# One more, smaller group in a grouped pipeline: images in groups of 2, 2, 6 x 4, 2, 2 instead of 2, 7 x 4, 2

## The chip, the cores and the metric

The kernel runs on one core of a Trainium2 chip, as one launch. The metric is the device time of that launch in microseconds (us), as the median over several runs. An engine is called here by the profile's name: PE (TensorE), DVE (VectorE), ACT (ScalarE), POOL (GpSimd), SP (SyncE). An image has 68 positions (36 patches and 32 text tokens) of 256 features; 32 images make 2176 rows, which are 17 tiles of 128 rows.

## The reference, cut to what matters

Four layers with residual sums: windowed attention, a mixture of 64 experts with 8 chosen per row, a layer that mixes the positions of an image by a learned causal roll, and a mixture of 8 experts with one chosen per row. The change lies in the third layer, which is this:

```python
z = softmax(einsum('bse,he->bsh', x, W_A) * SCALING, axis=1)     # per image and head, over positions
roll = transpose(z)[:, :, (i - j) % S] * (j <= i)                # causal roll
v = einsum('bse,fe->bsf', x, W_V).reshape(B, S, H, D)
out = einsum('bhij,bjhd->bihd', roll, v).reshape(B, S, E)
h = h + einsum('bse,fe->bsf', out, W_O) + b_O                    # x is layernorm(h)
```

The kernel computes the roll as a convolution: a discrete Fourier transform over the 68 positions of an image (two real matrices, `fwd`), products with the transform of z, and the inverse (`inv`). Ahead of it stands the end of the second layer: each row of h gets the weighted sum of the 8 rows that its experts left in memory. Behind it stand the layernorm and the 8 router logits of the fourth layer.

## The kernel before, in words

The third layer is one function, `roll_layer` (from line 1503), with an instruction list of its own for each engine, and every wait is written out by hand. The 32 images are cut into groups (`SIZES`, line 1510: 2, then seven times 4, then 2). All five engines go through the same rounds i = 0, 1, ..., `STEPS` - 1, where `STEPS` is the number of groups and three more (12 before). In round i

- group i is collected: DVE adds the 8 expert rows to each tile (`combine`, line 1948) and measures it for the layernorm (`measure`);
- group i-1 is normalised by ACT, transposed by PE (`turn("in")`, line 1635), and gets its logits z (`mix_logits`, 1643), its values v (`values`, 1654, one pair of images at a time), the softmax over z (`mix_shift` and `mix_norm` on DVE) and the transform of z (`turn_mix`, `forward_mix`);
- group i-2 gets the transform of v (`forward`, line 1663, two matmuls per pair), the products (`multiply`, line 2008, on DVE), the inverse (`invert`, line 1690) and the projection (`project`, line 1701);
- group i-3 gets the residual sum, the second layernorm, a transpose (`turn("out")`, also line 1635) and the router logits (`choose`, line 1736), and SP stores its tiles (lines 1599 and 1600).

Images don't end where tiles do. A group collects the tiles that its last image reaches (`tiles_in`), and hands out the tiles that are then complete (`tiles_out`). Before, `tiles_in` is 0 1 | 2 3 | 4 5 | 6 7 | 8 9 | 10 11 | 12 13 | 14 15 | 16, and `tiles_out` is 0 | 1 2 | 3 4 | 5 6 | 7 8 | 9 10 | 11 12 | 13 14 | 15 16.

POOL issues the 136 gathers of the expert rows (line 1623), 8 per tile in order of tiles, whatever the groups are. The buffer holds four tiles, so the gathers of tile t wait for the sums of tile t-4. In its first gathers POOL also waits for the end of the second layer's shared expert, whose last 9 tiles PE, ACT and DVE work off before round 0.

DVE, in a round (lines 2031 to 2077): the scale of the "in" norm, the residual sum, the "out" measures, the products of the first pair, the scale of the "out" norm, the bias, the sums of all collected tiles but the last, the softmax's shift, the products of the second pair, the softmax's norm, and at the end the sums of the last collected tile. PE, in a round (lines 1766 to 1825): the forward transforms, matmuls on idle data that only keep it running (`fill`, line 1712: 6 in a steady round of 4 images, 20 in rounds 1 and 2), the "in" transposes, logits, values, the "out" transposes, values of the second pair, router logits, the two inverses, `turn_mix`, `project`, `forward_mix`. Outside the steady rounds (`steady(g)`: 1 < g < NG - 1) there are more such idle matmuls (`fill_mid`, `fill_values`).

SP issues four loads of 1 MiB of the fourth layer's weights ahead of the stores of group 4 (`if g == 4`, line 1593), that is once the tiles of group 3 are out. The fourth layer begins when all engines have left the block.

Of the kernel before, what the change touches and what calls it, by code (L numbers as in the profile page):

```python
# [851 lines left out]
def attention_and_mixture_0(nc, a, k):  # L852

    with ExitStack() as st:
        sb = lambda n, s, d=fp32: k["sb"](f"m0_{n}", s, d, st)
        x_rows = nc.dram_tensor("m0_x_rows", (T, D), fp32).ap()
        y_rows = nc.dram_tensor("m0_y_rows", (SLOTS0 * P, D), fp32).ap()
        coef = sb("coef", [P, NT, E0])
        ids = sb("ids", [P, SLOTS0], u32)
        tile_expert_row = sb("tile_expert_row", [1, 2 * P], i32)  # L860
        r = places(k, st, "m0", E0, K0, SLOTS0)
        shared_up, shared_down = sb("shared_up", [P, DC, 2 * D]), sb("shared_down", [P, DC, D])
        with ExitStack() as js:
            jb = lambda n, s, d=fp32: k["sb"](f"m0_{n}", s, d, js)
            m = dict(coef=coef, ids=ids, tile_expert_row=tile_expert_row, x_rows=x_rows,
                     router=jb("router", [P, DC, E0]), e_bias=jb("e_bias", [P, E0]),
                     up=shared_up, down=shared_down)
            m["routing_in"], = sems(nc, k, "m0j", "routing_in")
            aT = jb("aT", [P, DC, T])
            wo = jb("wo", [P, DC, D])  # L870
            window_attention(nc, a, k, m, aT, wo)
            join_and_route(nc, k, m, r, aT, wo)
        wt = sb("wt", [P, NT, K0])
        expert_tiles_0(nc, a, k, ids, tile_expert_row, x_rows, y_rows, r, coef, wt)
        clear_sems(nc, k)
        roll_layer(nc, a, k, r, wt, y_rows, shared_up, shared_down)
# [626 lines left out]
def roll_layer(nc, a, k, r, wt, y_rows, shared_up, shared_down):  # L1503
# [3 lines left out]
    fwd = [k["const"]("fwd_re"), k["const"]("fwd_im")]  # L1507
    inv = [k["const"]("inv_re"), k["const"]("inv_neg"), k["const"]("inv_im"), k["const"]("inv_im")]
    GI, PAIR = 4, 2
    SIZES = [2] + [4] * 7 + [2]  # L1510
    assert sum(SIZES) == B
    NG = len(SIZES)
    FROM = [sum(SIZES[:g]) for g in range(NG + 1)]
    GC = GI * S
# [13 lines left out]
    def halves(g):  # L1528
        return range(SIZES[g] // PAIR)

# [6 lines left out]
    def cols_of(g):  # L1537
        return slice(FROM[g] * S, FROM[g + 1] * S)
# [13 lines left out]
    with ExitStack() as st:  # L1552
# [35 lines left out]
        with nc.Block() as block:  # L1588
# [39 lines left out]
            def _(pe):  # L1628
# [9 lines left out]
                def mix_logits(g):  # L1638
# [3 lines left out]
                    for c in range(DC):  # L1642
                        mm = nc.tensor.matmul(pz[0:H, 0:SIZES[g] * S], late["w_a"][:, c, :], xT[:, c, cols_of(g)],
                                              start=(c == 0), stop=(c == DC - 1))
# [21 lines left out]
                def turn_mix(g):  # L1666
                    pe.wait_ge(z_normed, g + 1)
                    for b in range(SIZES[g]):
                        mm = nc.tensor.transpose(pz[0:S, b * H:(b + 1) * H], z[:, b, :], ident[0:H, 0:H])
# [814 lines left out]
```

## Time and profile before

| | us |
|---|---|
| median of 3 runs | 1057.34 (1054.91 to 1061.70) |
| the profiled execution, its own time | 1059.86 |
| its span | 1058.10 |
| PE busy in the span | 947.0 (90%) |
| DVE busy | 589.4 (56%) |
| POOL busy | 520.6 (49%) |
| roll layer, first gather to the router logits on DVE | 626.1 to 860.1 |

Times in the rows below are counted from the start of the span. A row of a timeline reads: start, duration, engine, line, operation, output tile <- input tiles, shape, how many instructions are merged; in square brackets the engine's idle time just before it and what ended that. PEclk is the clock that PE was granted: 1.00 is 2.4 GHz, 0.50 is 1.2 GHz.

### The profile page before, as it was taken

Reading aid. Unit: us, or ns where it says so; the run is one execution under the profiler, and the core shown is the slowest. Engines: PE = TensorE matmul, PEld = TensorE weight load, DVE = VectorE, ACT = ScalarE, POOL = GpSimd, SP = SyncE. Lnnn points to the kernel's source line nnn. Section 1 sums busy time; section 2 is a strip of 40 time slices with the busy share of each in tenths; the row PEclk is TensorE's granted clock in tenths of the full one; section 3 lists DMA queues with packets and bytes.
Section 4 is the critical chain, followed back from the end, with each engine's and each line's share of the span. In section 5 each row is a group of like instructions: output and inputs, shape, how many; then the busy total and the mean of one; then the engine's idle time right before and its main releaser. Section 6 shows DMA issues by size and latency. Waiting matters only on the chain. (4 is left out here: it accounts for less than half of the span.)

```text
span 1058.1 us, 29663 instructions
## 1 busy us (share of the span) xinstructions
PE 947.0 (90%) x10380; PEld 745.1 (70%) x10398; DVE 589.4 (56%) x1463; ACT 413.5 (39%) x1102; POOL 520.6 (49%) x714
## 2 busy tenths in 40 slices
PE   8899999988747999999999998789888957999996
PEld 6667777777634888888888876355556635888895
DVE  1778888865994777433333325676887551111111
ACT  2267677734243344444443422222333222333431
POOL 0055665610604777777777627777772002433432
PEclk9999999999969999999999999887999987999998
DMA  7010000002004888877788723344483056476650
GB/s 256 1 46 2 0 0 0 1 12 75 1 1 161 292 283 261 272 247 224 242 265 253 230 89 100 100 113 122 122 289 80 21 191 218 143 262 222 266 155 25
DMA packets 79820, 149.28 MB, mean 141 GB/s; under 512 B 18892, under 2 KB 53327, under 8 KB 75760
## 3 DMA queue, kind: packets, MB, share of 16 engines
q1 hardware_dynamic: 34768, 77.15, 21.7%
q0 software_dynamic: 17712, 47.88, 16.0%
q10 hardware_dynamic: 27248, 23.09, 6.5%
q8 instruction: 50, 0.82, 0.3%
q14 instruction: 42, 0.34, 0.1%
HBM read 200.22 MB, written 31.73 MB: 219 GB/s over the span
## 5 line engine op out<-in xcount | busy, mean ns | idle before, releaser
L1332 POOL DMA_INDIRECT x_x<-m_x_rows,x_idx x170 | 165.7, 975 | 75.1 <-issue 35.6
L1358 PE MATMUL x_pup<-x_xt,x_w 128*128 128x128 f32 (+1 forms) x2176 | 182.9, 250 | 0.0
L1358 PEld LDWEIGHTS x_pup<-x_xt,x_w 128*128 128x128 f32 (+1 forms) x2176 | 166.9, 165 | 5.9 <-issue 5.7
L1623 POOL DMA_INDIRECT rl_y<-m_y_rows,rl_idx x136 | 134.2, 986 | 43.6 <-issue 36.3
L1439 DVE TENSOR_TENSOR x_hid<-x_gate,x_pup 128x128 f32<-128x128 f32 x170 | 48.9, 288 | 148.3 <-ACT x_gate L1411 140.9
L1372 PE MATMUL x_pdown<-x_w,x_hid 128*128 128x256 f32 (+1 forms) x408 | 104.2, 389 | 0.3 <-DVE x_y L1446 0.3
L1407 ACT ACTIVATE x_xt<-x_pturn 128x256 f32<-128x256 f32 x170 | 65.3, 384 | 89.3 <-PE x_pturn L1343 86.2
L442 POOL TENSOR_TENSOR wa_probs<-wa_probs,wa_peak 68x544 f32<-68x544 f32 x64 | 69.9, 1092 | 57.6 <-DVE wa_peak L593 54.9
L2420 DVE TENSOR_TENSOR x_y<-x_pdown,x_b 128x256 f32<-128x256 f32 x21 | 8.9, 425 | 151.7 <-PE x_pdown L2374 151.7
L2406 ACT ACTIVATE x_hid<-x_pup,x_b 128x128 f32<-128x128 f32 (+1 forms) x200 | 52.8, 357 | 95.9 <-PE x_pup L2357 95.8
L1411 ACT ACTIVATE x_gate<-x_pup 128x128 f32<-128x128 f32 x170 | 47.2, 278 | 92.4 <-PE x_pup L1358 91.7
L1953 DVE SCALAR_TENSOR_TENSOR h<-rl_y,m_wt,h 128x256 f32<-128x256 f32 x136 | 66.2, 487 | 18.1 <-DMA rl_y<-m_y_rows,rl_idx 13.8
L1446 DVE COPY x_y<-x_pdown 128x256 f32<-128x256 f32 x170 | 71.3, 420 | 2.0 <-PE x_pdown L1372 0.5
L1343 PE MATMUL x_pturn<-cst,x_x 128*128 128x128 f32 x340 | 67.1, 279 | 4.6 <-DMA x_x<-m_x_rows,x_idx 4.6
L1343 PEld LDWEIGHTS x_pturn<-cst,x_x 128*128 128x128 f32 x340 | 44.8, 141 | 32.6 <-issue 13.1
L2313 POOL DMA_INDIRECT out_h<-x_y,m_ids_out x21 | 21.1, 1006 | 94.5 <-DVE x_y L2423 88.5
L637 ACT ACTIVATE wa_probs<-wa_probs 68x544 f32<-68x544 f32 x64 | 42.1, 658 | 46.3 <-POOL wa_probs L442 46.1
L1317 POOL COPY x_idx<-m_ids 128x1 uint32 (+1 forms) x170 | 36.9, 218 | 41.6 <-POOLq L921 40.5
L1372 PEld LDWEIGHTS x_pdown<-x_w,x_hid 128*128 128x128 f32 (+1 forms) x408 | 48.1, 173 | 3.9 <-DVE x_hid L1439 0.6
L2357 PE MATMUL x_pup<-x_xt,late_w 128*128 128x128 f32 x384 | 47.0, 282 | 4.1 <-ACT x_xt L2396 2.5
L2357 PEld LDWEIGHTS x_pup<-x_xt,late_w 128*128 128x128 f32 x384 | 45.9, 198 | 6.4 <-issue 4.1
L589 DVE TENSOR_TENSOR wa_probs<-wa_scores,cst 68x544 f32<-68x544 f32 x64 | 46.0, 719 | 5.2 <-PE wa_scores L542 2.7
(344 smaller groups left out, 1904.7 us busy)
## 6 DMA issues: line engine op xcount, KB each, us to landing
x_w<-in_experts SPq DMA_DIRECT2D x204, 384.0 KB
late_w<-in_w SPq DMA_DIRECT2D x28, 1024.0 KB
m_y_rows<-x_y ACTq DMA_DIRECT2D x170, 128.0 KB
xT<-in_w SPq DMA_DIRECT2D x12, 1024.0 KB, 6.0
xn<-in_w SPq DMA_DIRECT2D x10, 1024.0 KB, 10.3
h<-in_w SPq DMA_DIRECT2D x10, 1024.0 KB, 14.0
m_x_rows<-xn SPq DMA_DIRECT2D x34, 128.0 KB, 1.8
x_x<-m_x_rows,x_idx POOLq DMA_INDIRECT x170
```

The lines of the kernel that those rows point to most:

```text
L442: nc.gpsimd.tensor_tensor(probs[:, slot4, :, :], probs[:, slot4, :, :], peak[:, slot2, :].unsqueeze(2).broadcast_to([S, HC, S]), ALU.subtr ...
L1332: nc.gpsimd.indirect_dma_start(x[:, s, :], None, x_rows, bass.IndirectOffsetOnAxis(ap=idx[:, s:s + 1], axis=0))\
L1343: mm = nc.tensor.transpose(pturn[:, bank, c * P:(c + 1) * P], x[:, s, c * P:(c + 1) * P], ident)
L1358: mm = nc.tensor.matmul(pup[rows:rows + wide, bank, m * P + side * wide:m * P + (side + 1) * wide], w[:, lane, first:first + wide], xt[:, ...
L1372: mm = nc.tensor.matmul(pdown[rows, s % 2, 0:D], hid[:, s, rows], w[:, lane, UP:W], start=True, stop=True)
L1407: nc.scalar.activation(xt[:, s, :], pturn[:, bank, 0:D], ACT.Copy).then_inc(turn_moved, 1)
L1439: nc.vector.tensor_tensor(hid[:, s, :], gate[:, s, :], pup[:, bank, P:2 * P], ALU.mult)\
L1446: nc.vector.tensor_copy(y[:, s, :], pdown[:, s % 2, 0:D]).then_inc(down_moved, 1)
L1623: nc.gpsimd.indirect_dma_start(y[:, t % YR, kk, :], None, y_rows, bass.IndirectOffsetOnAxis(ap=idx[:, n:n + 1], axis=0))\
L1953: nc.vector.scalar_tensor_tensor(h[:, t, :], y[:, t % YR, kk, :], wt[:, t, kk:kk + 1], h[:, t, :], ALU.mult, ALU.add).then_inc(added, 1)
L2357: mm = nc.tensor.matmul(pup[rows:rows + wide, s, half, to:to + wide], w1[l][:, c, first:first + wide], xt[:, s, at:at + wide], start=(c == ...
L2406: ins = nc.scalar.activation(hid[:, s, f, side * wide:(side + 1) * wide], pup[:, s, f // HB, at:at + wide], ACT.Gelu, bias=b1[:, l, f:f + 1])
```

## The change

Only the list of group sizes differs. The number of groups goes from 9 to 10, and so `STEPS` from 12 to 13; everything else follows from the list.

```diff
-    SIZES = [2] + [4] * 7 + [2]
+    SIZES = [2, 2] + [4] * 6 + [2, 2]
     assert sum(SIZES) == B
     NG = len(SIZES)
```

`tiles_in` becomes 0 1 | 2 | 3 4 | 5 6 | 7 8 | 9 10 | 11 12 | 13 14 | 15 | 16, and `tiles_out` 0 | 1 | 2 3 | 4 5 | 6 7 | 8 9 | 10 11 | 12 13 | 14 | 15 16. The steady rounds are those in which group i-1 is one of 2 to 8 (2 to 7 before); a steady round whose group i-1 has 2 images gets 3 idle matmuls instead of 6.

## Rows read from the trace of the kernel before

**Rows 1.** The page's costliest groups: the gathers on POOL.

```profile
L1623 POOL DMA_INDIRECT rl_y<-m_y_rows,rl_idx x136 | 134.2, 986 | 43.6 <-issue 36.3
```

**Rows 2.** Timeline of POOL: last of the 8 gathers of tiles 5, 8, 12.

```profile
689.17 0.95 POOL L1623 DMA_INDIRECT rl_y<-m_y_rows,rl_idx  x1 [0.30 <-issue]
...
719.89 0.95 POOL L1623 DMA_INDIRECT rl_y<-m_y_rows,rl_idx  x1 [0.30 <-issue]
...
761.30 0.94 POOL L1623 DMA_INDIRECT rl_y<-m_y_rows,rl_idx  x1 [0.30 <-issue]
```

**Rows 3.** Timeline of DVE: the sums of tiles 5, 6 and 16.

```profile
691.91 4.15 DVE L1953 SCALAR_TENSOR_TENSOR h<-rl_y,m_wt,h 128x256 f32<-128x256 f32 x8 [3.00 <-DMA rl_y<-m_y_rows,rl_idx]
...
702.75 4.19 DVE L1953 SCALAR_TENSOR_TENSOR h<-rl_y,m_wt,h 128x256 f32<-128x256 f32 x8 [1.06 <-DMA rl_y<-m_y_rows,rl_idx]
...
820.09 4.11 DVE L1953 SCALAR_TENSOR_TENSOR h<-rl_y,m_wt,h 128x256 f32<-128x256 f32 x8
```

**Rows 4.** Timeline of PE: round 6, and the start of round 7.

```profile
764.45 2.75 PE L1663 MATMUL rl_pf<-rl_v,cst 68*68 68x512 f32 x6
...
768.33 0.38 PE L1635 MATMUL rl_pt<-cst,xn 128*128 128x128 f32 x2
769.28 0.41 PE L1635 MATMUL rl_pt<-cst,xn 128*128 128x128 f32 x2 [0.56 <-ACT xT L1867]
...
775.02 1.89 PE L1654 MATMUL rl_pv<-late_w_v,xT 128*68 128x256 f32 x8
776.74 0.95 PE L1736 MATMUL rl_po<-late_wr,rl_x 128*128 128x8 f32 x8
...
780.34 2.12 PE L1690 MATMUL rl_po<-cst,rl_term 68*64 68x68 f32 x64 [0.59 <-ACT xT L1832]
...
782.95 1.99 PE L1701 MATMUL rl_pr<-late_w_o,xT 128*128 128x256 f32 x8 [0.25 <-ACT xT L1832]
...
785.02 2.74 PE L1663 MATMUL rl_pf<-rl_v,cst 68*68 68x512 f32 x6
```

**Rows 5.** Table by stretch: length, PE busy (instructions), PEclk, DMA share, GB/s.

```profile
660.00:667.00 7.00, 2.39 (x13) 0.94 0.35 100
667.00:676.00 9.00, 8.78 (x22) 0.50 0.37 104
...
700.00:704.00 4.00, 3.93 (x10) 0.57 0.52 154
...
711.00:726.00 15.00, 14.63 (x89) 0.50 0.38 107
726.00:760.00 34.00, 29.31 (x305) 0.98 0.49 132
```

**Rows 6.** Timeline of PE: rounds 3 and 4 (first transposes, and the second inverse).

```profile
698.18 0.44 PE L1635 MATMUL rl_pt<-cst,xn 128*128 128x128 f32 x2 [2.21 <-ACT xn L1861]
...
710.84 3.90 PE L1690 MATMUL rl_po<-cst,rl_term 68*64 68x68 f32 x64 [0.95 <-DVE rl_term L2008]
...
726.94 0.63 PE L1635 MATMUL rl_pt<-cst,xn 128*128 128x128 f32 x2
```

**Rows 7.** Timeline of PE: round 9, and the start of round 10.

```profile
826.15 2.74 PE L1663 MATMUL rl_pf<-rl_v,cst 68*68 68x512 f32 x6
...
839.51 2.12 PE L1690 MATMUL rl_po<-cst,rl_term 68*64 68x68 f32 x64
...
845.18 1.88 PE L1663 MATMUL rl_pf<-rl_v,cst 68*68 68x512 f32 x4
```

**Rows 8.** Timeline of DVE: the router logits, the roll layer's last work.

```profile
859.83 0.30 DVE L2079 TENSOR_TENSOR logit<-rl_po,late_br 128x136 f32<-128x136 f32 x1 [3.64 <-PE rl_po L1736]
```

**Rows 9.** Timeline of SP: the first of four 1 MiB weight loads.

```profile
773.21 0.44 SPq L1595 DMA_DIRECT2D late_w<-in_w  x1
```

**Rows 10.** Table by stretch while they run: length, POOL busy, PEclk, DMA, GB/s.

```profile
780.00:784.00 4.00, 3.08 (x4) 1.00 1.02 402
```

**Rows 11.** Chain that ended last: a gather of the fourth layer.

```profile
973.53 6.52 DMA x_x<-m_x_rows,m_ids
```

**Rows 12.** Table by stretch, all engines: length, busy of PE, PEld, DVE, ACT, POOL, PEclk.

```profile
765.38:785.95 20.57, 18.07 (x195) 12.00 (x195) 18.06 (x43) 7.45 (x20) 15.70 (x17) 1.00 0.77 258
```

## The prediction

> **What bounds the kernel now.** I read the page first, then the timelines of POOL, DVE and PE over the roll layer, side by side, then a table of PE's clock by stretch, and last the chain of waits. The change touches one layer of 234 us, so the question is what sets that layer's end.
>
> Three rates meet there. *The gathers.* POOL issues 136 of them, 986 ns each, and nearly all its idle time is its own issue gap [rows 1]. The last gather of tile 8 starts at 719.89 and that of tile 12 at 761.30, so a tile takes 10.35 us, two tiles 20.7 us [rows 2]. *PE's list.* In a steady round (four images, two tiles in, two out) PE goes from one forward transform to the next in 785.02 - 764.45 = 20.57 us [rows 4], with only short waits for ACT. *DVE* is busy 18.06 of those 20.57 us [rows 12] and waits for ACT in the rest. So gathers and PE run at almost the same rate, and what counts is how far the compute lags behind the gathers.
>
> Early on it doesn't lag: the sums of tiles 5 and 6 begin after DVE has waited 3.00 and 1.06 us for the DMA [rows 3]. Late it does: the last gather of the layer is out about 4 tiles of 10.35 us after tile 12's, at some 802.7, and the sums of tile 16 start only at 820.09, without a wait [rows 2, 3].
>
> Where does the lag come from? PE's clock. It is at half speed (0.50, 1.2 GHz) from 667 to 676, low (0.57 on average) from 700 to 704 and at half again from 711 to 726; from 726 on it is full [rows 5]. Each fall follows light work: PE was busy 2.39 of 7 us before the first, stood idle 2.21 us ahead of the transposes of round 3 and 0.95 us ahead of an inverse [rows 5, 6]. The last fall costs most. From that inverse to the first transpose of the next round PE took 726.94 - 710.84 = 16.10 us [rows 6]; the same piece of a steady round is (785.02 - 780.34) + (768.33 - 764.45) = 8.56 us [rows 4]. So a microsecond at half clock loses 7.54 / 16.10 = 0.47 us.
>
> **The change part by part.** I call the start of the first forward transform of round i its mark M(i). Before, M(9) = 826.15, and the layer ends at 859.83 [rows 7, 8].
>
> *What stays.* POOL's order, its DMAs and their number; the sums, inverses, projections, transposes and stores by tile or pair. The four-tile buffer holds POOL up no more than before, since no tile is summed later than the gathers four tiles on need it. SP issues the same 34 stores, cut otherwise.
>
> *What is added.* One round: one more `turn_mix` and `forward_mix`, a pair of small ACT operations for the norms, softmax steps over 2 images. I don't price these one by one; they lie in the lengths of the rounds below. No wait is added to any queue.
>
> *The early rounds.* Rounds 1 to 4 now collect tile 2; 3 and 4; 5 and 6; 7 and 8. Tile 6 ends a group now, tile 5 did before. The first transpose of the next round follows the start of the last tile's sums by 698.18 - 691.91 = 6.27 us [rows 3, 6], so round 4's transposes come at 702.75 + 6.27 = 709.0. From there to the next mark a steady round needs 785.02 - 768.33 = 16.69 us [rows 4]. Round 4 hands out one tile instead of two: less one transpose (769.28 - 768.33 = 0.95) and half of the router logits (0.95 / 2): 15.3. M(5) = 724.3 at full clock. The gathers allow it: sums can start 691.91 - 689.17 = 2.74 us after the last gather's start [rows 2, 3], so tile 8 gives transposes at 719.89 + 2.74 + 6.27 = 728.9, and, less the 3.88 from mark to transpose, M(5) = 725.0. Both together: 725.
>
> *The steady rounds.* From M(5) to M(9) four rounds of 20.57 = 82.3 us if PE sets the pace. The gathers ask for M(7) no earlier than 761.30 + 2.74 + 6.27 - 3.88 = 766.4 (PE alone: 725 + 41.1 = 766.1), M(8) 20.7 later. So M(9) = 766.4 + 20.7 + 20.57 = 807.7 at full clock.
>
> *The late rounds.* Round 9 takes in group 8 (2 images, one tile) and works off group 7 (4 images): a steady round less one transpose (0.95), less the second pair's values (776.74 - 775.02 = 1.72), less half the idle matmuls (six take 768.33 - 764.45 - 2.75 = 1.1, so 0.55) [rows 4]: 17.3. Round 10 is the old round 9, 845.18 - 826.15 = 19.03 [rows 7], less the second pair: two of its transforms (2.74 / 3 each, 1.8), an inverse (2.12) with its two idle matmuls (0.4), and one tile's projection (1.99 / 2): 13.7. Round 11 to the end is the old stretch from M(10), 859.83 - 845.18 = 14.65, less what a transpose and logits of one tile (1.4) save where PE's idle matmuls end about 0.5 late: 14.2. Together 45.2 after M(9), where before it was 33.7. The added round thus costs 11.5 us behind M(9), and the compute must be that much ahead at M(9): it gains if M(9) is under 859.83 - 45.2 = 814.6, that is if M(5) is under 732.3.
>
> *PE's clock.* Rounds 2 and 3 now hold one pair of images to work off. Round 3 is a steady round less 1.8 of transforms, 2.7 of inverse with its wait, 1.4 of a tile out and 1.0 of projection, 13.7 us of work, while two tiles of gathers take 20.7. So PE stands idle some 6 us ahead of round 3 and again ahead of round 4, more than the 2.21 us after which the clock fell before [rows 6]. I expect half clock at the start of round 4, the first dense one. The spells in the trace are about 3, 9 and 15 us [rows 5]; they cost 1.6, 4.2 and 7.1. Below nothing the price can't go, since before that stretch also ran partly at half. I take the middle spell, which like the new round 4 follows a long thin stretch: M(5) = 724.3 + 4.2 = 728.5, M(9) = 810.8, end 856.0, 3.8 us earlier than 859.83.
>
> The Trainium skill speaks against the change here: TensorE: Matmul & The Clock Gate, section "HAM oscillation — how this bites in real kernels", says that matmul work cut into pieces shorter than the wait for the next piece makes the clock fall at each piece, so that each next one begins slow, and advises larger pieces. The trace agrees for the early rounds (0.50 and 0.57 behind the idle times above); by it rounds 3 and 4 would both begin at half clock, the slower rival below.
>
> *The weight loads.* Before, SP issues them at 773.21, 8.8 us after M(6) [rows 9, 4]; now M(6) = 749.1 and they start near 758, while the gathers of tile 12 are out. They fill the DMA engines (402 GB/s) [rows 10]. Before, the tiles gathered meanwhile had slack. Now a late landing would show. Bounds: none, or the 6.52 us that a gather of the fourth layer took beside weight loads [rows 11] in place of 2.74, so 3.8 us. The upper end gives M(7) = 766.4 + 3.8 = 770.2; with the clock spell M(7) is 728.5 + 41.1 = 769.6 already. So the two hide behind each other, and I add nothing.
>
> *After the layer.* The fourth layer starts behind a barrier and moves as a whole. So 3.8 us come off the profiled execution's own 1059.86, to 1056.1; the median of the runs shown lies 2.5 lower, so I predict 1053.5.
>
> **The rivals.**
> - *Full clock.* The half-clock spells fall into idle time, and the gathers alone set the pace: end 807.7 + 45.2 = 852.9, 6.9 us gained, 1050.4. For it: the first spell before lay in slack. Against: round 4 is dense and follows an idle stretch.
> - *Long spell.* As from 711 to 726: 7.1 us, M(5) = 731.4, 0.9 us gained, 1056.4. The head start pays for the extra round and nothing is left.
> - *Slower: the clock falls twice.* Round 4 runs at half for a long spell (7.1) and another round, still waiting for gathers, for a middle one (4.2): M(5) would in effect be 735.6, past 732.3, from where the extra round costs more than it brings. 3.3 us lost, 1060.6. For it: the thin rounds, and two falls within 12 us before. Against: once PE lags it has no long idle time, and the clock was steady from 726 on.
> - *The weight loads decide* at full clock: M(7) = 770.2, end 770.2 + 20.57 x 2 + 45.2 = 856.5, 3.3 us gained, 1054.0. It can't be told from the forecast by the time, only by a DVE wait on a DMA.
>
> **How the numbers follow.** Forecast 0.42, weight loads 0.10 (the same time), full clock 0.16, long spell 0.10, slower 0.22. Forecast and weight loads have a range of their own of 1051 to 1056. From full clock (1050.4, and 2 for the spread of runs) to the slower rival (1060.6, and 1) the range is 1048 to 1062. A measurement of this kernel tells about 1%, 10.6 us, from no change. None of the cases reaches that; more falls of the clock than I count, or a layer that also gains elsewhere, would have to add to it. Faster by over 1%: 0.05; within: 0.88; slower by over 1%: 0.07.
>
> **What would show it right or wrong.** Right: the sums of tiles up to 7 or 8 still wait for DMA; M(5) near 728 to 729; rounds of 20.57 to M(9) near 811; then some 45 us to the end near 856; half clock somewhere between 705 and 725. Wrong step by step: M(5) near 725 with PEclk 1.00 (full clock); M(5) over 732 (slower); a DMA wait on DVE near 765 to 770 (weight loads); rounds 9 to the end far from 45.2 (my sum of the tail). A gather rate other than 10.35 us a tile would make all of it wrong.

## The result and the profile after

The changed kernel takes 1065.75 us (median of 14 runs, 1059.18 to 1071.11), the kernel before 1060.16 in the same comparison (14 runs, 1054.91 to 1068.45). The ratio is 1.0055 [1.0028, 1.0082]: slower by about half a per cent, where 0.4% faster was forecast. The profiled execution after has an own time of 1061.45 and a span of 1059.7, only 1.6 above the span before. That is one draw, so what follows compares the roll layer alone, from the start of its first gather to its router logits, and all marks M(i) below count from that first gather.

The page after has the gathers as they were: 136 of them, 976 ns each (986 before, [rows 1]).

```profile
L1623 POOL DMA_INDIRECT rl_y<-m_y_rows,rl_idx x136 | 132.8, 976 | 43.5 <-issue 37.5
```

The timeline of POOL after, the layer's first gather and the last one of tile 12:

```profile
624.37 0.96 POOL L1623 DMA_INDIRECT rl_y<-m_y_rows,rl_idx  x1 [0.42 <-POOL rl_idx L1606]
...
758.84 0.95 POOL L1623 DMA_INDIRECT rl_y<-m_y_rows,rl_idx  x1 [0.30 <-issue]
```

The timeline of DVE after, the sums of tile 12 and the router logits:

```profile
767.82 4.15 DVE L1953 SCALAR_TENSOR_TENSOR h<-rl_y,m_wt,h 128x256 f32<-128x256 f32 x8 [4.21 <-DMA rl_y<-m_y_rows,rl_idx]
...
864.14 0.30 DVE L2079 TENSOR_TENSOR logit<-rl_po,late_br 128x136 f32<-128x136 f32 x1 [3.22 <-PE rl_po L1736]
```

So the layer takes 864.14 - 624.37 = 239.8 us. Before, its first gather started at 626.05, so with [rows 8] it took 233.8. The layer alone lost 6.0, close to the 5.6 between the medians; the rest of the profiled execution was 4.4 shorter by chance or by what stands around the layer.

Where in the layer? The timeline of PE after gives the marks (L1663, six or four instructions at once), the first transposes of rounds 4 and 7 (L1635) and the inverses of round 9 (L1690):

```profile
706.29 0.69 PE L1635 MATMUL rl_pt<-cst,xn 128*128 128x128 f32 x2 [2.19 <-ACT xn L1861]
...
727.18 2.74 PE L1663 MATMUL rl_pf<-rl_v,cst 68*68 68x512 f32 x6
...
747.76 2.74 PE L1663 MATMUL rl_pf<-rl_v,cst 68*68 68x512 f32 x6
...
771.55 2.74 PE L1663 MATMUL rl_pf<-rl_v,cst 68*68 68x512 f32 x6
...
775.43 0.38 PE L1635 MATMUL rl_pt<-cst,xn 128*128 128x128 f32 x2
...
812.68 2.74 PE L1663 MATMUL rl_pf<-rl_v,cst 68*68 68x512 f32 x6
...
822.40 3.90 PE L1690 MATMUL rl_po<-cst,rl_term 68*64 68x68 f32 x64
826.89 3.89 PE L1690 MATMUL rl_po<-cst,rl_term 68*64 68x68 f32 x64 [0.59 <-ACT xT L1832]
...
835.25 2.22 PE L1663 MATMUL rl_pf<-rl_v,cst 68*68 68x512 f32 x4
...
849.91 1.88 PE L1663 MATMUL rl_pf<-rl_v,cst 68*68 68x512 f32 x4
```

M(5) comes at 727.18 - 624.37 = 102.8, where before it was 117.8: the head start was 15 us. M(9) comes at 188.3 instead of 200.1, so 11.8 of it is left. From M(9) to the end before needs 33.7 [rows 7, 8], after 51.5. The balance is 11.8 - 17.8 = -6.0.

Two rounds stand out. Round 6, from 747.76 to 771.55, took 23.8 where the steady round has 20.57 [rows 4]. Round 9, from 812.68 to 835.25, took 22.6. In it each inverse (64 matmuls of L1690) takes 3.90 us, in a steady round 2.12: that is the half clock. The table of PE by stretch (length, PE busy (instructions), PEclk, DMA share, GB/s) shows it in both rounds, and in rounds 3 and 4 before them:

```profile
686.00:690.00 4.00, 2.96 (x8) 0.50 0.36 104
706.00:710.00 4.00, 2.67 (x7) 0.52 0.33 101
720.00:726.00 6.00, 5.86 (x66) 0.50 0.31 90
...
760.00:764.00 4.00, 3.41 (x84) 1.00 0.88 328
764.00:768.00 4.00, 3.70 (x65) 0.53 1.01 401
768.00:772.00 4.00, 4.00 (x14) 0.62 1.02 397
772.00:776.00 4.00, 3.81 (x14) 1.00 0.82 296
...
821.00:835.00 14.00, 13.03 (x150) 0.54 0.03 11
```

The first three lines are spells of rounds 3 and 4; the forecast had priced one, in round 4. The one in round 3 ended before PE waited 2.19 us ahead of round 4's transposes, so it cost nothing there. The spell from 764 to 772 lies where the DMA engines are full and the sums of tile 12 wait 4.21 us for their gather. The last one, 821 to 835, fills round 9 with almost no DMA traffic at all. The timeline of SP after has the first of the four weight loads just ahead of the spell in round 6:

```profile
756.52 0.45 SPq L1595 DMA_DIRECT2D late_w<-in_w  x1
```

The wait of 4.21 us on DVE did not reach PE in this profile: the transposes of round 7 start at 775.43, the usual 3.88 behind the mark, with no wait. What lengthened round 6 is the half clock alone. At full clock PE would have waited for tile 12 some 1.9 us (767.82 + 6.27 [rows 3, 6] against 747.76 + 20.57 + 3.88), by an estimate from these rows.

### The profile page after: what moved, and what is told of

It is laid out like the page before. It is cut to its first block and busy times, and to the rows that moved or that the text cites. A ratio compares the mean times of both kernels' runs of the same rounds, so it can differ in the third digit from the quotient of the medians.

```text
span 1059.7 us, 29719 instructions
## 1 busy us (share of the span) xinstructions
PE 951.3 (90%) x10405; PEld 749.8 (71%) x10405; DVE 590.6 (56%) x1471; ACT 414.3 (39%) x1110; POOL 519.9 (49%) x714
## 5 line engine op out<-in xcount | busy, mean ns | idle before, releaser
L1953 DVE SCALAR_TENSOR_TENSOR h<-rl_y,m_wt,h 128x256 f32<-128x256 f32 x136 | 66.1, 486 | 16.1 <-DMA rl_y<-m_y_rows,rl_idx 11.8
## 6 DMA issues: line engine op xcount, KB each, us to landing
xn<-in_w SPq DMA_DIRECT2D x10, 1024.0 KB, 10.1
```

What stands on the lines that cost most here:

```text
L1953: nc.vector.scalar_tensor_tensor(h[:, t, :], y[:, t % YR, kk, :], wt[:, t, kk:kk + 1], h[:, t, :], ALU.mult, ALU.add).then_inc(added, 1)
```

## The experiments

The theory after this reading: two costs beyond the forecast, one of the weight loads (round 6) and one of a clock spell in the thin round 9. The rivals: that the regroup costs its extra round whatever is mended, that the early clock spells decide, and that the weight loads are hidden. Every kernel of this part was timed in five rounds, 12 runs, against the kernel before (a run of e2 at 1076.39 us, far above its others, is left out of the ratio). In the table the marks, the layer and the stretch from M(9) to the end are from one profile each, in us; "loads late" means the four weight loads ahead of the stores of group 6 instead of group 4.

| kernel | ratio to before [95%] | M(5) | M(9) to end | layer |
|---|---|---|---|---|
| before | 1 | 117.8 | 33.7 | 233.8 |
| after | 1.0055 [1.0028, 1.0082] | 102.8 | 51.5 | 239.8 |
| e1: after, round 9 filled | 1.0039 [1.0013, 1.0066] | 100.7 | 47.4 | 236.2 |
| e2: after, loads late | 1.0018 [0.9989, 1.0046] | 100.9 | 51.4 | 234.6 |
| e3: after, early idle matmuls | 1.0029 [1.0002, 1.0057] | 105.2 | 51.4 | 241.9 |
| e4: after, all three | 0.9992 [0.9964, 1.0019] | 101.0 | 47.5 | 230.8 |
| f1: after, round 9 filled, loads late | 0.9989 [0.9960, 1.0017] | 101.6 | 47.5 | 231.6 |
| f2: f1, more idle matmuls early | 0.9988 [0.9954, 1.0023] | 101.6 | 47.5 | 231.4 |
| b1: before, loads late | 0.9961 [0.9931, 0.9990] | 111.3 | 33.7 | 230.4 |
| b2: before, early idle matmuls | 1.0036 [1.0010, 1.0061] | 119.2 | 33.7 | 238.2 |
| g1: before, loads late, gaps filled | 0.9937 [0.9912, 0.9962] | 109.9 | 33.7 | 227.4 |
| g2: f1, gaps filled | 0.9950 [0.9926, 0.9974] | 98.8 | 47.5 | 229.8 |
| g3: before, gaps filled | 0.9985 [0.9964, 1.0006] | 110.3 | 33.7 | 233.9 |

**Round 9 filled (e1).** A round counts as steady by the group it takes in, and in a steady round no idle matmuls stand between the transposes and inverses. The edit takes group 8 out, so that round 9 gets them:

```diff
-                    return 1 < g < NG - 1
+                    return 1 < g < NG - 2
```

> The changed kernel, with the idle matmuls of the unsteady rounds also in round 9 (group 8 counted as unsteady). Clock theory: in the changed kernel PE falls to half clock from about 821 to 836, in the thin round 9, and that costs 5 of the 6 us by which its roll layer is longer; with idle matmuls PE stays at 1.00 there, round 9 takes 18.5 to 19.5 us instead of 22.6, and the time falls by 3 to 4 us against the changed kernel, to a ratio of about 1.002 to the kernel before. Round theory (the extra round costs its own length whatever the clock does): the idle matmuls only add about 1.7 us, ratio 1.006 to 1.008. Loads theory (the weight loads in round 6 are the main cost): round 9 hardly matters, ratio 1.004 to 1.006.

The timeline of PE of this kernel, round 9:

```profile
813.79 2.74 PE L1663 MATMUL rl_pf<-rl_v,cst 68*68 68x512 f32 x6
...
824.12 2.12 PE L1690 MATMUL rl_po<-cst,rl_term 68*64 68x68 f32 x64
...
832.82 1.88 PE L1663 MATMUL rl_pf<-rl_v,cst 68*68 68x512 f32 x4
```

The table of PE by stretch over the same round:

```profile
818.00:832.00 14.00, 13.24 (x174) 1.00 0.12 39
```

The clock stays full, the inverse is back at 2.12, and the round takes 832.82 - 813.79 = 19.0 instead of 22.6, although it holds more matmuls. The stretch from M(9) to the end falls from 51.5 to 47.4. The ratio falls less, to 1.0039 where about 1.002 was expected, and its interval overlaps that of after: the gain is plain in the profile and not in the time. That profile has a longer wait for tile 12, 5.78 us on DVE, and here it reaches PE, 1.33 us ahead of round 7's transposes. The timelines of DVE and PE:

```profile
768.57 4.14 DVE L1953 SCALAR_TENSOR_TENSOR h<-rl_y,m_wt,h 128x256 f32<-128x256 f32 x8 [5.78 <-DMA rl_y<-m_y_rows,rl_idx]
...
774.85 0.44 PE L1635 MATMUL rl_pt<-cst,xn 128*128 128x128 f32 x2 [1.33 <-ACT xn L1861]
```

**The loads late (e2).**

```diff
-                    if g == 4:
+                    if g == 6:
```

> The changed kernel, with the four weight loads two rounds later, ahead of the stores of group 6, when all gathers are issued. Loads theory: the sums of tile 12 no longer wait 4.2 us for their DMA, round 6 takes 20.6 us instead of 23.8, the time falls by 3 us against the changed kernel, ratio about 1.0025 to the kernel before. Clock theory: the round 9 spell remains; the wait goes but what is won may be lost to it again, ratio 1.002 to 1.0055. Round theory: no change, ratio 1.0055. If the loads now land too late for the fourth layer, its first matmuls wait and the ratio is above 1.006.

The timeline of PE of this kernel: the marks of rounds 6, 7 and 9, and round 9's slow inverse:

```profile
746.63 2.74 PE L1663 MATMUL rl_pf<-rl_v,cst 68*68 68x512 f32 x6
...
767.20 2.74 PE L1663 MATMUL rl_pf<-rl_v,cst 68*68 68x512 f32 x6
...
808.34 2.74 PE L1663 MATMUL rl_pf<-rl_v,cst 68*68 68x512 f32 x6
...
818.01 3.89 PE L1690 MATMUL rl_po<-cst,rl_term 68*64 68x68 f32 x64
...
830.85 2.30 PE L1663 MATMUL rl_pf<-rl_v,cst 68*68 68x512 f32 x4
```

The table of PE by stretch, where after had its spell of round 6:

```profile
760.00:776.00 16.00, 14.06 (x172) 1.00 0.38 109
```

Round 6 is 767.20 - 746.63 = 20.57 again, at full clock, and DVE's wait for tile 12 is at most 0.44. Round 9 is still 22.5. So this profile is without the one cost and has the other. By the ratios the edit is worth 1.0055 - 1.0018 = 0.37%, 3.9 us; the two intervals still overlap.

**Idle matmuls early (e3).** More of them ahead of the transposes of rounds 3 and 4, to hold the clock there:

```diff
-                        fill(g1, 6 * SIZES[g1] // GI if steady(g1) else 20 if g1 < 2 else 4)
+                        fill(g1, 26 if 1 < g1 < 4 else 6 * SIZES[g1] // GI if steady(g1) else 20 if g1 < 2 else 4)
```

> The changed kernel, with 26 idle matmuls instead of 6 ahead of the transposes of rounds 3 and 4, where PE now stands idle 4.5 and 2.2 us. Clock theory: the half clock from 685 to 692, 706 to 713 and 720 to 726 goes, the mark of round 5 comes 103 - 4 = 99 us after the first gather instead of 102.8. What then follows tells two cases apart: with the loads theory the wait for tile 12 grows by what was won, and the ratio stays at 1.0055; without it the ratio falls to about 1.002. Round theory: nothing to win early, ratio 1.0055 or higher.

A miss. The timeline of PE of this kernel, the idle matmuls ahead of round 3's transposes and the first transforms of round 4:

```profile
681.49 5.78 PE L1712 MATMUL rl_pz<-m_chosen_b,m_before_b 128*128 128x512 bf16 x26
...
701.97 5.33 PE L1663 MATMUL rl_pf<-rl_v,cst 68*68 68x512 f32 x6
```

The 26 idle matmuls ran for 5.78 us, and the six transforms 14.7 us after their end still took 5.33 instead of 2.74, at half clock. M(5) came at 105.2, no earlier than after, and the ratio of 1.0029 can't be told from that of after. Of the clock this profile is one draw: e4 has the same block in the same place, and in its timeline of PE the same six transforms took 2.74:

```profile
699.95 2.74 PE L1663 MATMUL rl_pf<-rl_v,cst 68*68 68x512 f32 x6
```

**All three (e4), and the two that work (f1).** Both carry the edits of e1 and e2; e4 has that of e3 too.

> All three edits on the changed kernel. Clock and loads theory together: PE at 1.00 from round 3 on, no wait for tile 12, mark of round 5 at 99 us after the first gather, four rounds of 20.6 to 20.7, 46 to 47 us from the mark of round 9 to the router logits: a layer of 228 us, where it was 234.1 before and 240.1 after; 6 us under the kernel before, ratio 0.994. Round theory: the extra round still costs, ratio 1.000 to 1.004.

> The changed kernel, with the idle matmuls in round 9 and the weight loads two rounds later, but without the early idle matmuls. Two-cost theory (round 9's half clock and the wait for tile 12 are separate costs of some 3.5 us each, and the early idle matmuls brought nothing): as the kernel with all three edits, ratio 0.998 to 1.000, a layer of 231 us. If the early idle matmuls carried part of it: ratio 1.001 to 1.003. If the two costs hide behind each other: no better than either alone, ratio 1.002 to 1.004.

0.9992 and 0.9989 are one result: the early idle matmuls carried nothing. Both profiles have 20.6 to 20.8 in each round from 5 to 8 and 19.0 in round 9, so the two costs are separate and add up. By the ratios f1 is 0.66% under after, 7 us, and the intervals are apart; the round 9 edit alone is worth 0.16% (after to e1) to 0.29% (e2 to f1). That brings the new groups back to the time of the kernel before and not below it. In e4 the clock still fell once, in round 4, where the timeline of PE has a wait for DVE ahead of an inverse:

```profile
719.16 3.12 PE L1690 MATMUL rl_po<-cst,rl_term 68*64 68x68 f32 x64 [1.01 <-DVE rl_term L2008]
```

**More idle matmuls early (f2).** f1 with the early rounds out of the steady ones, so that they too have idle matmuls in between:

```diff
-                    return 1 < g < NG - 2
+                    return 3 < g < NG - 2
...
-                        fill(g1, 6 * SIZES[g1] // GI if steady(g1) else 20 if g1 < 2 else 4)
+                        fill(g1, 6 * SIZES[g1] // GI if steady(g1) else 20 if g1 < 2 else 14 if g1 < 4 else 4)
```

> As the kernel with all three edits, but with idle matmuls also within rounds 3 and 4 (groups 2 and 3 counted as unsteady) and 14 instead of 26 ahead of their transposes. Clock theory: the fall that remained in round 4 (0.50 from about 720 to 727, behind a wait of 1.0 us in mid-round) goes too, and the mark of round 5 comes at 98 instead of 101 us after the first gather; a layer of 228 us, ratio 0.996. If gathers bound that stretch, or the idle matmuls themselves hold the round up: mark of round 5 at 100 to 103, ratio 0.998 to 1.001.

The clock fell once (0.64 from 710 to 714) and was full from about 88 us into the layer on, and still M(5) came at 101.6, inside the range of the second case. Which half of that case holds shows beside g2, a kernel further below, whose M(5) is 98.8. The timelines of PE of f2 and then of g2, the first transposes of round 4 and M(5):

```profile
709.71 0.44 PE L1635 MATMUL rl_pt<-cst,xn 128*128 128x128 f32 x2 [2.10 <-ACT xn L1861]
...
728.50 2.74 PE L1663 MATMUL rl_pf<-rl_v,cst 68*68 68x512 f32 x6
...
706.96 0.44 PE L1635 MATMUL rl_pt<-cst,xn 128*128 128x128 f32 x2 [3.14 <-ACT xn L1875]
...
723.82 2.74 PE L1663 MATMUL rl_pf<-rl_v,cst 68*68 68x512 f32 x6
```

Counted from the first gather (626.86 in f2, 624.99 in g2), the transposes come at 82.9 and 82.0, so the gathers make 0.9 of the difference; from there to M(5) f2 takes 18.8 and g2 16.9, with the idle matmuls that f2 has added to that round between its other work. So in f2 the idle matmuls held the round up more than the gathers did, and there was something left to win: g2 won it.

**The kernel before with the same edits (b1, b2).** Were the two costs the change's own? b1 moves the loads as e2 does. b2 puts idle matmuls ahead of the transposes of rounds 3 and 4, as e3 does:

```diff
-                        fill(g1, 6 * SIZES[g1] // GI if steady(g1) else 20 if g1 < 2 else 4)
+                        fill(g1, (16, 12)[g1 - 2] if 1 < g1 < 4 else 6 * SIZES[g1] // GI if steady(g1) else 20 if g1 < 2 else 4)
```

> The kernel before, with only the weight loads two rounds later. Loads theory as I hold it (before, the compute lags the gathers by some 6 us, so the loads delayed nothing): ratio 1.000, 0.998 to 1.002. Rival (the loads cost the kernel before as much, and moving them is the whole gain of the kernel with all three edits): ratio 0.996 or lower.

> The kernel before, with 16 and 12 idle matmuls instead of 6 ahead of the transposes of rounds 3 and 4. Clock theory: the half clock from 700 to 704 and 711 to 726 goes in most runs, the mark of round 5 comes at 110 to 112 instead of 117.8 us after the first gather, and since nothing behind it waits the whole is kept: a layer of 227 to 229 us, ratio 0.994 to 0.996, so that the old groups with a steady clock beat the new ones. Rival (the clock falls for another reason than idle time ahead of the transposes, as with the 26 idle matmuls on the changed kernel, where it fell in round 4 all the same): mark of round 5 at 116 to 119, ratio 0.999 to 1.001.

Two misses. b1 is faster than before, 0.9961, so by the times the loads cost the old groups about as much (0.39%) as the new ones (0.37%, after to e2): as far as the intervals tell, they are a cost of both kernels and don't account for the difference between them. Its one profile doesn't show how: its gain is already there at M(5) (111.3 instead of 117.8), before the loads are issued in either kernel, and it has a spell of its own in round 6. b2 is slower, 1.0036. The table of PE by stretch has it at full clock through the transposes of round 3, where before had a spell from 700 to 704 [rows 5]:

```profile
676.00:708.00 32.00, 28.96 (x239) 1.00 0.39 108
```

But then the clock falls all the same, behind a wait of 2.46 us for DVE in the middle of the round, as the timeline of PE shows:

```profile
710.02 3.89 PE L1690 MATMUL rl_po<-cst,rl_term 68*64 68x68 f32 x64 [2.46 <-DVE rl_term L2008]
...
718.43 5.33 PE L1663 MATMUL rl_pf<-rl_v,cst 68*68 68x512 f32 x6
```

These two also show that where a spell falls changes from run to run: b1 has one in round 6 and b2 one in round 7, where before had none. The tables of PE by stretch of b1 and then of b2:

```profile
773.00:780.00 7.00, 6.86 (x72) 0.51 0.37 104
...
802.00:809.00 7.00, 6.86 (x70) 0.51 0.14 40
```

Both rounds take 23.6, as long as round 6 of after, and no weight load is moving in either spell. So a spell of this kind in a steady round doesn't need the loads, and a single profile is one draw of them. The mean clocks of whole runs say the same: among the 14 of the changed kernel the four fastest have 0.960 to 0.967, the four slowest 0.952 to 0.955.

**Gaps filled (g1, g2, g3).** Idle matmuls not ahead of the work but in PE's short waits inside the steady rounds: one behind the transpose of each tile in, one behind that of the first tile out, two behind the first inverse. The waits in the two new helpers are for buffers that the idle matmuls overwrite.

```diff
+                def idle_mid(g, n):
+                    pe.wait_ge(z_moved, g + 1)
+                    for _ in range(n):
+                        nc.tensor.matmul(pz[:, :], r["before_b"][:, :], filler, start=True, stop=True)
+
+                def idle_values(g, n):
+                    pe.wait_ge(v_moved, pairs_through(g))
+                    for _ in range(n):
+                        nc.tensor.matmul(pv[:, :, :].rearrange("p b n -> p (b n)"), r["before_b"][:, :], filler,
+                                         start=True, stop=True)
...
                         turn("in", t)
-                        if not steady(g1):
-                            fill(g1, 1)
+                        fill(g1, 1)
...
                         turn("out", t)
+                        if steady(g1) and t == outs[0]:
+                            idle_mid(g1, 1)
...
                         fill_values(g1, 2)
+                        if steady(g1):
+                            idle_values(g1, 2)
```

g1 is b1 with this edit, g2 is f1 with it, g3 is before with it and the loads where they were.

> The kernel before with the weight loads two rounds later and, in the steady rounds, idle matmuls inside PE's waits for ACT: one behind each of the first transposes and two between the inverses, where PE waits 0.47 to 0.59 us anyway. Clock theory: a steady round stays at 20.6 to 20.8 us and the clock falls in fewer runs; a layer of 226 to 229 us, ratio 0.992 to 0.995, with runs closer together. If the spells come from elsewhere: as with the loads alone, ratio 0.995 to 0.998.

> The changed groups with the late loads, the idle matmuls in round 9 and the same idle matmuls in PE's waits. Two theories of what the groups are worth once clock and loads are out of the way: head start against extra round (15 us of head start at the mark of round 5, 13.7 us for the extra round): within 0.002 of the same edits on the kernel before, that is 0.993 to 0.997. Groups gain once the clock is steady (the prediction's full-clock case): ratio below that of the same edits on the kernel before by 0.003 or more.

> The kernel before with only the idle matmuls in PE's waits, the weight loads where they were. If those loads cost the kernel before only when its compute doesn't lag the gathers: with a steady clock a wait of 2 to 5 us for the DMA shows in round 6 or 7, and the ratio is 0.996 to 0.999, above that of the kernel with late loads as well by 0.003 or so. If the loads cost nothing there: no wait, and the same ratio as with late loads.

g1 takes 1053.61 us (12 runs, 1050.45 to 1059.29), 0.9937 [0.9912, 0.9962]: faster than both kernels. The timeline of PE of g1, two inverses of round 5 with the idle matmuls in between:

```profile
727.76 2.12 PE L1690 MATMUL rl_po<-cst,rl_term 68*64 68x68 f32 x64
729.82 0.60 PE L1722 MATMUL rl_pv<-m_chosen_b,m_before_b 128*128 128x512 bf16 x2
730.48 2.12 PE L1690 MATMUL rl_po<-cst,rl_term 68*64 68x68 f32 x64
```

The timeline of DVE of g1 (its lines stand 14 further down), sums and router logits:

```profile
754.67 4.15 DVE L1967 SCALAR_TENSOR_TENSOR h<-rl_y,m_wt,h 128x256 f32<-128x256 f32 x8 [3.01 <-DMA rl_y<-m_y_rows,rl_idx]
...
852.70 0.30 DVE L2093 TENSOR_TENSOR logit<-rl_po,late_br 128x136 f32<-128x136 f32 x1 [3.65 <-PE rl_po L1747]
```

From 80 us into the layer on the clock doesn't fall any more, and the sums wait for the gathers (3.01): the compute no longer lags, as it did in [rows 3]. The table of PE by stretch, late in the layer:

```profile
776.00:800.00 24.00, 22.74 (x215) 1.00 0.45 122
```

g3 differs from g1 only in the loads. Its timeline of DVE:

```profile
781.30 4.15 DVE L1967 SCALAR_TENSOR_TENSOR h<-rl_y,m_wt,h 128x256 f32<-128x256 f32 x8 [7.13 <-DMA rl_y<-m_y_rows,rl_idx]
```

its timeline of PE:

```profile
787.58 0.69 PE L1635 MATMUL rl_pt<-cst,xn 128*128 128x128 f32 x2 [4.87 <-ACT xn L1875]
```

and its table of PE by stretch just after:

```profile
786.00:794.00 8.00, 6.23 (x18) 0.59 0.45 131
```

This is the whole chain in three lines: the weight loads delay a gather, DVE waits 7.13 for it, PE stands idle 4.87, and PE comes back at half clock. The round, its round 7, takes 27.4 instead of 20.6. g3 is at 0.9985, g1 at 0.9937, with intervals that don't overlap, so the loads cost the old groups 0.48% here, about 5 us. The filled gaps themselves are worth 0.15% (before to g3), 0.24% (b1 to g1) and 0.39% (f1 to g2), the same way each time, though in each pair the intervals overlap.

**What the grouping itself costs.** With each edit on both groupings, the new groups against the old: 1.0055 against 1; with the loads late 1.0018 against 0.9961, 0.57% apart where the first pair is 0.55%; with the loads late and the new round 9 filled 0.9989 against 0.9961; with all gaps filled as well 0.9950 against 0.9937. In the last two pairs the intervals overlap. So by the times about half of what the change cost went with round 9's half clock and half stayed, and neither half by itself is clear of the noise. In no pair are the new groups ahead.

## Why the prediction was wrong

- *The gathers: right, a little slow.* From tile 12's last gather (758.84) to tile 16's (799.33) a tile took 10.1 us where 10.35 was counted on, and with the clock held (g1) the sums wait for them again.
- *The early rounds and the clock there: right in kind, and in the number by some luck.* M(5) was forecast at 728.5 - 626.05 = 102.45 behind the first gather and came at 102.8, with half clock in round 4 where it was looked for. But it fell twice in that round, and from the first transposes to M(5) the round took 727.18 - 706.29 = 20.9, where 15.3 + 4.2 = 19.5 was forecast; the transposes themselves came 1.0 earlier than forecast (81.9 behind the first gather, not 83.0). In g2, where the clock in that round was better, M(5) is 98.8, near the 725 - 626.05 = 98.95 of the full-clock case.
- *The steady rounds: right* in three of four: 20.6 in rounds 5, 7 and 8.
- *"So the two hide behind each other, and I add nothing": wrong in the sum.* This is the step on the weight loads, and round 6 took 3.2 us more than it allowed. The upper bound itself was too low: tile 12's sums began 767.82 - 758.84 = 8.98 after its last gather's start, not at most 6.52. Yet that wait did hide, as the step said, though behind another spell than the one it meant. What it left out is the spell, from 764 to 772, since the clock was priced once. In the profiles of the new groups with early loads (after, e1, e3), the clock is down between 764 and 776 in three of three, in those with late loads (e2, e4, f1, f2, g2) in none of five, which speaks for the loads; b1 and b2 have the same spell without them, which speaks for chance. In g3 the spell follows a wait; in after the clock was down before PE had a long wait, and why it fell there stays open.
- *"Round 9 takes in group 8 … 17.3": wrong, and the larger miss.* The 17.3 was a steady round less its parts, at full clock. The round ran at half for most of its length and took 22.6, 5.3 more. It fell in all three profiles that left round 9 as it was (after, e2, e3: 22.5 to 22.6) and in none of the five that filled its waits (e1, e4, f1, f2, g2: 19.0). The step subtracted a transpose, values and three idle matmuls and kept the full clock, as if the clock did not depend on them. With idle matmuls put back it held, and 19.0 is the price; what made it fall without them is not shown.
- *Round 10: 13.7 forecast, 14.7 measured*, the rest of the spell in its first transforms (2.22 instead of 1.88) and a small miss of the subtraction: with round 9 filled it is 14.2. *Round 11 to the end: right*, 14.2.
- The terms add up: 0.35 at M(5), 3.2, 5.3 and 1.0 make 9.9, and the layer was forecast at 856.0 - 626.05 = 229.95 and took 239.8. The time missed by 12.25 us (1065.75 against 1053.5). Most of the rest is the 2.5 us taken off because the median of three runs lay that far under the profiled execution: over 14 runs the kernel before has 1060.16, no less than its profiled 1059.86.
- *The break-even.* The extra round was put at 11.5 behind M(9). It costs 51.5 - 33.7 = 17.8 with the half clock and 47.5 - 33.7 = 13.8 without. The head start at M(9) was 11.8 in after, and without the loads' cost 196.7 - 184.1 = 12.6 (b1 against f1) and 193.7 - 182.3 = 11.4 (g1 against g2). So in these profiles even a clean round costs more than the smaller first group brings, by 1.2 to 2.4 us; the times of the two pairs agree, but not clear of the noise.
- *The rivals.* "The clock falls twice" had the direction and the kind of cost. Its falls in rounds 3 and 4 did come, but M(5) was only 0.35 later than forecast; those that made the change slower came in rounds 6 and 9. The reason given against it, that the clock was steady from 726 on, read steadiness off four-image rounds and carried it to a two-image round. "The weight loads decide" was right as to a wait on DVE, and its time was not: in after that wait cost PE nothing, and the rival had no half clock in it.

The rule of the Trainium skill named in the prediction (TensorE: Matmul & The Clock Gate, "HAM oscillation — how this bites in real kernels") was applied to rounds 3 and 4 only. There the trace agrees: in after the clock was 0.50 from 686 to 690 behind a wait of 4.51 us, and 0.52 from 706 to 710 behind one of 2.19, and both times the work behind the wait began slow. In round 9 the waits on PE are under 0.6 us each, and the clock fell all the same (0.54).

## What to carry to other kernels

A smaller first and last group shortens the lead-in but adds a round to the drain; price that round from a thin round's own row, with the clock that it had there, before counting on a steady round less its parts. Here idle matmuls paid in the short waits inside the rounds (three pairs, 0.15 to 0.39%) and did not as a block ahead of the transposes (e3, b2), and bulk loads were better issued late, where hardly a gather was still due (four pairs, 0.37 to 0.50%). When runs of one kernel spread by 10 us and the change is worth 5, apply the same edit to both versions: the pairs here showed that the loads cost both groupings alike, which the profiles of before and after did not.

## What the runs showed of the hardware that was not expected

- In round 9 of after PE was busy 13.03 of 14 us at a granted clock of 0.54, and the clock did not recover until the next round. It fell there without a wait of 0.6 us or more on PE. The same round with idle matmuls in its waits (e1) stayed at 1.00.
- A block of 26 idle matmuls, 5.78 us long, did not settle the clock: the next round's six transforms took 5.33 at half clock in e3 and 2.74 in e4. One or two in the short waits of the steady rounds (g1) went with a full clock from 80 us into the layer to its end. What makes the clock fall was not found.
- Four loads of 1 MiB and the gathers beside them moved 401 GB/s together, and the sums of tile 12 could start only 8.98 us after its last gather's start, where it was 2.74 without loads [rows 2, 3]. In g3 DVE waited 7.13 us for a tile so delayed.
